# A decoder layer on one core: the null key and value subtracted in the fold, scores in two banks, gate in the banks of the transposes

## The reference

```
x = x + q * scan(sigmoid(a), kv)             # [q, kv, a] = norm(layernorm(x)) @ w_qkva
x = x + layernorm(attention(layernorm(x), context)) * ln_scale + ln_bias
x = x + bitlinear(silu(bitlinear(xn, w_gate)) * bitlinear(xn, w_up), w_down)   # xn = layernorm(x)
```

```
k = concat(null_k, k); v = concat(null_v, v)       # 65 rows
attn = softmax(q k^T / 8);  out = concat_heads(attn v) @ Wout
```

## Time and profile before

| what | value |
|---|---|
| three runs | 515.12, 511.77, 512.62 us; median 512.62 |
| span of the profiled execution | 510.8 us (the profile gives no other time of it) |
| PE busy | 476.4 us, 93% |
| DVE busy | 416.6 us, 82% |
| ACT busy | 334.4 us, 65% |
| POOL busy | 314.1 us, 61% |
| chain that ended last | PE 74%, DVE 11%, POOL 4%, DMA 3%, issue 3% |

### The profile page before, as it was taken

The page is one execution under the profiler, slowest core; times in us unless marked ns, Lnnn a source line. Parts: engine busy times, 40 slices in busy tenths (PEclk is TensorE's granted clock), DMA queues, the critical chain, the costliest instruction groups (busy, mean ns, idle before and its releaser), DMA issues.

```text
span 510.8 us, 8856 instructions
## 1 busy us (share of the span) xinstructions
PE 476.4 (93%) x2934; PEld 390.5 (76%) x2962; DVE 416.6 (82%) x933; ACT 334.4 (65%) x461; POOL 314.1 (61%) x486
## 2 busy tenths in 40 slices
PE   1999999999997998999999999999999999999774
PEld 0778888877676887888888888888888888887432
DVE  4789898968437558799999899898998998997786
ACT  3556652245333334788888888888897888787562
POOL 2234546510003457788787887887878778788861
PEclk9999999999999999999999999999999999999979
DMA  8996000320000000011122211313132212221234
GB/s 256 324 360 255 3 0 1 72 52 2 0 1 1 1 1 7 6 27 42 36 52 45 50 39 38 58 42 49 36 50 46 53 37 52 44 52 37 63 85 117
DMA packets 67116, 31.80 MB, mean 62 GB/s; under 512 B 49664, under 2 KB 65280, under 8 KB 67072
## 3 DMA queue, kind: packets, MB, share of 16 engines
q1 hardware_dynamic: 67072, 31.24, 24.5%
HBM read 15.24 MB, written 4.19 MB: 38 GB/s over the span
## 4 chain that ended last, share of the span: by engine, by line
PE 74%; DVE 11%; POOL 4%; DMA 3%; issue 3%; SPq 2%; ACT 2%; DVEq 0%; POOLq 0%; ACTq 0%
PE psum L1270 33%; PE psum L1534 10%; PE psum L1539 9%; PE psum L1286 9%; DMA xs<-in_x_dram 3%; PE psum L1510 2%; PE psum L1518 2%; SPq L397 2%; PE psum L1412 2%; PE psum L1391 1%; PE psum L1305 1%; DVE den L1080 1%; PE psum L1374 1%; DVE region_d L1071 1%; DVE mx L1068 1%
## 5 line engine op out<-in xcount | busy, mean ns | idle before, releaser
L554 POOL TENSOR_TENSOR region_d<-region_d,rden 128x1024 f32<-128x1024 f32 x32 | 60.9, 1903 | 74.9 <-DVE rden L1085 74.9
L1270 PE MATMUL psum<-Mhi,xT2hi 128*128 128x260 f32 x256 | 75.9, 297 | 0.2
L1270 PE MATMUL psum<-Mlo,xT2hi 128*128 128x260 f32 x256 | 72.9, 285 | 0.0
L1270 PE MATMUL psum<-Mhi,xT2lo 128*128 128x260 f32 x256 | 72.9, 285 | 0.0
L1534 PE MATMUL psum<-VW,region_d 128*128 128x256 f32 x256 | 61.2, 382 | 3.2 <-DVE pTn L1174 3.2
L1539 PE MATMUL psum<-VW,region_d 128*128 128x256 f32 x256 | 60.5, 379 | 0.0
L1534 PEld LDWEIGHTS psum<-VW,region_d 128*128 128x128 f32 x256 | 48.3, 191 | 13.1 <-DVE pTn L1174 4.5
L1068 DVE TENSOR_REDUCE mx<-psum 128x8 f32<-128x520 f32 x64 | 44.5, 696 | 13.0 <-PE psum L1270 11.4
L1539 PEld LDWEIGHTS psum<-VW,region_d 128*128 128x128 f32 x256 | 48.6, 190 | 6.6
L1093 DVE SCALAR_TENSOR_TENSOR region_c<-psum,zw,region_c 128x1024 f32<-128x1024 f32 x32 | 41.0, 1283 | 12.5 <-ACT region_c L768 10.9
L1270 PEld LDWEIGHTS psum<-Mhi,xT2hi 128*128 128x128 f32 x256 | 48.7, 190 | 1.3 <-issue 0.9
(11 more groups left out here) (151 smaller groups left out, 1217.5 us busy)
## 6 DMA issues: line engine op xcount, KB each, us to landing
out_dram<-xs SPq DMA_DIRECT2D x32, 128.0 KB, 1.9
xs<-in_x_dram SPq DMA_DIRECT2D x1, 2560.0 KB, 13.4
VW<-in_L_xattn_Wkv_dram SPq DMA_DIRECT2D x1, 2048.0 KB, 12.2
region_b<-in_L_xattn_Wkv_dram SPq DMA_DIRECT2D x1, 2048.0 KB, 18.4
xs<-in_x_dram SPq DMA_DIRECT2D x3, 512.0 KB, 7.4
region_w<-in_L_ffn_w_gate_dram SPq DMA_DIRECT2D x2, 512.0 KB, 10.3
region_w<-in_L_ffn_w_up_dram SPq DMA_DIRECT2D x2, 512.0 KB, 7.7
region_w<-in_L_ffn_w_down_dram SPq DMA_DIRECT2D x8, 128.0 KB, 5.1
```

What stands on the lines that cost most here:

```text
L554: pool.tensor_tensor(p2[:, v, 0:H * MK].rearrange("p (h j) -> p h j", j=MK), e[:, :, 0:MK], rden[:, v, :].unsqueeze(2).broadcast_to([P, H, ...
L1270: mm = pe.matmul(dst, lhsT, rhs, start=i == 0, stop=i == len(terms) - 1)
```

## The change: what it does

With the null key subtracted from every key, the null score is 0, and softmax is the same: all scores of a row shift by one number. With the null value subtracted from every value, the output lacks a constant row, the null value times Wout, since the probabilities sum to 1. So ACT's copy in `put_kvT` becomes one with a bias, minus the null key or value of each row:

```diff
-                act.activation(kvT[:, i % 4, :], bank(i % 2, BM), ACT.Copy).then_inc(kvT_ready, 1)
+                null = 0 if i < HC else 1
+                act.activation(kvT[:, i % 4, :], bank(i % 2, BM), ACT.Identity, bias=nulls_neg[:, null:null + 1]) \
+                    .then_inc(kvT_ready, 1)
```

The 65th columns go: scores have 64 columns a head, 8 heads fill a bank, and a tile's scores are 12 matmuls of 128x512 into banks 0 and 1. Softmax shifts by max(maximum, 0) in one instruction that gives shift minus score, ACT's exponential has scale -1, and a small DVE instruction writes the null column of both halves:

```diff
             def softmax_half(n, hh, u):
 
-                scores = banks(2 * hh, 2)[:, :, 0:HB * J].rearrange("p b (h j) -> p b h j", j=J)
+                scores = bank(hh).rearrange("p (h j) -> p h j", j=MK)
+                e = e2[:, u, hh * HB * J:(hh + 1) * HB * J].rearrange("p (h j) -> p h j", j=J)
                 dve.wait_ge(sim_psum, 2 * n + hh + 1)
                 if hh == 0:
-                    if positive(2 * n - 2):
-                        dve.wait_ge(p_ready, 2 * n - 2)
-                dve.tensor_reduce(mx[:, hh, :].rearrange("p (b h) -> p b h", h=HB), scores, AX.X, ALU.max) \
-                    .then_inc(max_done, 1)
+                    if positive(n):
+                        dve.wait_ge(shift_done, n)
...
-                dve.tensor_tensor(
-                    e2[:, u, hh * 2 * HB * J:(hh + 1) * 2 * HB * J].rearrange("p (b h j) -> p b h j", b=2, j=J),
-                    scores,
-                    mx[:, hh, :].rearrange("p (b h) -> p b h", h=HB).unsqueeze(3).broadcast_to([P, 2, HB, J]),
-                    ALU.subtract).then_inc(sim_sub, 1)
+                if hh == 1:
+                    null = e2[:, u, :].rearrange("p (r h j) -> p r h j", r=2, j=J)[:, :, :, MK]
+                    dve.tensor_scalar(null, mx[:, :, :], 0.0, None, ALU.max).then_inc(shift_done, 1)
+                dve.scalar_tensor_tensor(out=e[:, :, 0:MK], in0=mx[:, hh, :].unsqueeze(2).broadcast_to([P, HB, MK]),
+                                         scalar=0.0, in1=scores, op0=ALU.max, op1=ALU.subtract).then_inc(sim_sub, 1)
```

The constant row is added on TensorE by a product of ones with `vnull` (hi part in one row, rest in another), now the first of the products in bank 7; the null transpose, its copies and the last product go:

```diff
@@ -1517,27 +1498,27 @@
                         at = (HC // 2 + i) * P
                         mm = pe.transpose(psum[:, 5, i * P:(i + 1) * P], p2[:, u, at:at + P], ident[:, :])
                     mm.then_inc(pT1_psum, 1)
-                    if positive(n):
-                        pe.wait_ge(y2_ready, n)
-                    if n == 0:
-                        pe.wait_ge(vwn_ready, 1)
-                    pe.transpose(psum[0:NP, 7, D:D + P], p2[:, u, H * MK:], ident[:, :]).then_inc(pTn_psum, 1)
                 if filling(n):
                     scores_half(n + 2, 1, (u4 + 2) % 4, half(n + 2 - u), batch(n + 2))
                 if exists(n + 2, T) and exists(n - 5, T):
                     gate_up(n, v)
                 if exists(n, T):
 
-                    pe.wait_ge(pTn_ready, n + 1)
+                    if positive(n):
+                        pe.wait_ge(y2_ready, n)
+                    if n == 0:
+                        pe.wait_ge(vnull_ready, 1)
+                    pe.matmul(bank(7, D), ones_r[:, :], vnull[:, :], start=True, stop=False)
                     pe.wait_ge(pT0_ready, n + 1)
                     for pair in range(HC // 2):
...
 
                     pe.wait_ge(pT1_ready, n + 1)
                     for pair in range(HC // 2, HC):
-                        pe.matmul(bank(7, D), pT[:, pair, :], VW[:, batch(n), pair, :], start=False, stop=False)
-                    pe.matmul(bank(7, D), pTn[:, :], VWnull[:, :], start=False, stop=True).then_inc(out_psum, 1)
+                        mm = pe.matmul(bank(7, D), pT[:, pair, :], VW[:, batch(n), pair, :], start=False,
+                                       stop=pair == HC - 1)
+                    mm.then_inc(out_psum, 1)
```

`vnull` is made by one matmul from the sum of Wout over the pairs of heads, which POOL forms:

```diff
             groups(stage1)
+            pool.wait_ge(nvsel_zero, 1)
+            for row in (0, DH // 2):
+                pool.tensor_copy(nvsel[:, row:row + 1], nulls[:, 1:2]).then_inc(nv_set, 1)
+            pool.wait_ge(wout_loaded, 16)
             pool.wait_ge(q_psum, NG)
-            pool.memset(nvsel, 0.0).then_inc(nvsel_zero, 1)
+            pool.tensor_tensor(wsum, wout[:, 0, :], wout[:, 1, :], ALU.add).then_inc(wout_summed, 1)
+            for pair in range(2, HC):
+                pool.wait_ge(wout_summed, pair - 1)
+                pool.tensor_tensor(wsum, wsum, wout[:, pair, :], ALU.add).then_inc(wout_summed, 1)
...
-            def null_values(first, end):
-
-                pe.wait_ge(nv_set, 2 * HC)
-                for pair in range(first, end):
-                    mm = pe.matmul(psum[0:NP, 7, 0:D], nvsel[:, pair * NP:(pair + 1) * NP], wout[:, pair, :],
-                                   start=pair == 0, stop=pair == HC - 1)
-                return mm
+            def null_values():
+
+                pe.wait_ge(nv_set, 2)
+                pe.wait_ge(wout_summed, HC - 1)
+                pe.matmul(psum[0:NR, 7, 0:D], nvsel[:, :], wsum, start=True, stop=True).then_inc(vnull_psum, 1)
```

`null_key` and the 16 copies of `null_values` go from DVE's part of the fold (removed functions, L995 to L1018), and with them the waits on them. Scores keep banks 0 and 1, up has banks 2 and 3, gate takes banks 4 and 5 behind the copies of T0 and T1 in the tiles up to n = 29, and stands behind up:

```diff
@@ -1444,22 +1416,14 @@
             def scores_half(n, hh, u4, q, b):
 
                 pe.wait_ge(xT2_lo_ready, q + 1)
-                if n == 0 and hh == 1:
-                    pe.wait_ge(vw_first, HC)
-                    pe.wait_ge(vw_second, HC)
                 if positive(2 * n - 1 + hh):
                     pe.wait_ge(sim_sub, 2 * n - 1 + hh)
-                if positive(n - 7):
-                    pe.wait_ge((silu_ready, h_ready)[hh], n - 7)
-                for g in (2 * hh, 2 * hh + 1):
-                    mm = group(bank(g, HB * J),
-                               [(xT[:, (u4 // 2) % 2, k, (u4 % 2) * P:(u4 % 2 + 1) * P],
-                                 m[:, k, b, g * HB * J:(g + 1) * HB * J])
-                                for k in range(KD) for xT, m in ((xT2hi, Mhi), (xT2hi, Mlo), (xT2lo, Mhi))])
-                mm.then_inc(sim_psum, 1)
+                group(bank(hh), [(xT[:, (u4 // 2) % 2, k, (u4 % 2) * P:(u4 % 2 + 1) * P],
+                                  m[:, k, b, hh * HB * MK:(hh + 1) * HB * MK])
+                                 for k in range(KD) for xT, m in ((xT2hi, Mhi), (xT2hi, Mlo), (xT2lo, Mhi))]) \
+                    .then_inc(sim_psum, 1)
 
...
+                if positive(n - 4):
+                    pe.wait_ge(silu_ready, min(n - 4, T - 7))
...
             def gate_up(n, slot, down_between=None):
 
                 pe.wait_ge(nT_ready[slot], 16 * ((n - 5) // 2 + 1))
-                pe.wait_ge(sim_sub, upto(2 * n + 5, 2 * T))
+                def up():
+
+                    if positive(n - 5):
+                        pe.wait_ge(h_ready, n - 5)
+                    for j in range(2):
+                        mm = group(bank(2 + j), [(nT3[:, slot, k, :], wuT[:, k, j * 512:(j + 1) * 512]) for k in range(KD)])
+                    mm.then_inc(up_psum, 1)
+
+                if n < T - 2:
+                    up()
+                else:
+                    pe.wait_ge(sim_sub, 2 * T)
                 if positive(n - 5):
                     pe.wait_ge(silu_ready, n - 5)
                 for j in range(2):
-                    mm = group(bank(j), [(nT3[:, slot, k, :], wgT[:, k, j * 512:(j + 1) * 512]) for k in range(KD)])
+                    if n < T - 2:
+                        pe.wait_ge((pT0_ready, pT1_ready)[j], n + 1)
+                    mm = group(bank(gate_bank(n) + j),
+                               [(nT3[:, slot, k, :], wgT[:, k, j * 512:(j + 1) * 512]) for k in range(KD)])
                 mm.then_inc(gate_psum, 1)
-                mm.then_inc(up_psum, 1)
+                if n >= T - 2:
+                    up()
...
                 if exists(n, T):
 
-                    pe.wait_ge(p_ready, 2 * n + 2)
+                    if n == 0:
+                        pe.wait_ge(vw_first, HC)
+                        pe.wait_ge(vw_second, HC)
+                    pe.wait_ge(p_ready, n + 1)
                     if positive(n):
                         pe.wait_ge(pT0_ready, n)
+                    if positive(n - 5):
+                        pe.wait_ge(silu_ready, min(n - 5, T - 7))
```

More of the change, by code:

```diff
@@ L1485, in gate_up @@
                     down(down_between, T)
-                pe.wait_ge(sim_sub, upto(2 * n + 6, 2 * T))
-                if positive(n - 5):
-                    pe.wait_ge(h_ready, n - 5)
-                for j in range(2):
-                    mm = group(bank(2 + j), [(nT3[:, slot, k, :], wuT[:, k, j * 512:(j + 1) * 512]) for k in range(KD)])
-                mm.then_inc(up_psum, 1)
+                if n >= T - 2:
+                    up()
             def stages2_3(n, u4):
```

186 lines of the change are left out of this document (77 added, 109 removed).

## The result

The changed kernel takes 498.62 us in the median of four runs (497.85 to 499.26) against 513.48 for the kernel before on the same occasion (511.77 to 515.12): 0.9701 of it, 95% interval 0.967 to 0.9731. The forecast was 497.5. The profiled execution after spans 496.7 us where the one before spans 510.8.

What follows compares the result with a forecast made beforehand. PE was taken as the bound, with DVE 6% behind. The terms 6.75 + 4.4 + 2.6 + 0.9 + 0.5 = 15.15 us off the 510.8 us span give 495.65, plus 1.8 for the median: 497.5 us, range 492 to 504.5.

Steps and rivals of the forecast that it cites:

- Steady tiles: Tiles n = 5 to 29, bound by PE: 0.27 us less a tile, 6.75 us in all (5.5 to 8.7).
- Merging: Scores on PE: twelve matmuls of 512 columns in place of 24 of 260 gain 0.16 us a tile (0.13 to 0.26).
- gate would cost no wait: Gate's second half, in its new place, follows ACT's copy of T1 with a slack of at least 0.24 us.
- the slower rival: DVE's fused difference takes two passes, 1.40 us in place of 0.70, and DVE becomes the bound: 521.0 us, chance 0.05.
- n = 1 to 4: Early tiles, where out mostly waits for DVE's null correction: -4.4 us (-2 to -5) once it goes.
- the null write: DVE's new write of the null column, 128x16, priced by a small product: +0.20 us a tile (0 to 0.28).
- n = 0: First tile: the second score half moves into PE's wait for the constant row: -2.6 us (-1.5 to -3.5).
- the half clock: PE's 1.2 GHz level in the first tile: lasting through out, it would cost up to 1.7 us more.
- The 0.36 us: In the first tile, out might start 0.36 us earlier, since POOL's small product no longer stands before DVE's release.
- Fold: Stretch before the first tile: less waiting for DVE's difference, -1.0, and -0.1 more, -0.9 us with the biases (0 to -1.3).
- the new wait of 1.6 us: On PE ahead of the last fold_values, a wait for ACT's copies replaces the eight null products, some 1.6 us.
- Tail: Tiles 30 and 31 give 2 x 0.27 us: -0.5 us (0 to -1.5).

Runs made afterwards that it cites:

- null_by_reduce: The changed kernel with the null write on DVE as a tensor_reduce in place of the tensor_scalar: 495.48 us, 0.9635 of the kernel before.
- after_again: The changed kernel unaltered, timed and traced again on another occasion: 499.06 us, 0.9698 of the kernel before.

## Why the prediction was right, and where its sizes were off

**Steady tiles.** The bound was read rightly: PE's own work, shown by a transposition that costs three quarters of its length and a DVE instruction of 0.69 us that costs nothing in the period. The term was 0.27 a tile and came as 0.293. Merging was sized well by the two pitches (0.16 against 0.14), though a matmul fewer saved 8.7 ns where the prediction read 12 to 14. From T1 to out a tile takes the same as before, 2.28 against 2.27, since the ones stand where the null transposition stood; what is gone is the null product behind out. From out's second half to the next scores an odd tile takes 2.52 in place of 2.65 and an even one 3.06 in place of 3.29; why the even ones, with `pair_T` there, gain 0.1 more stays open. That gate would cost no wait was right: in the tile that starts at 287.19 ACT's copy of T1 ends at 291.77 and gate's second half begins at 292.22, 0.45 later, where 0.24 at least was forecast, and the other order shows what the place is worth: 0.56 us of wait ahead of up, none behind it. The difference as a scalar_tensor_tensor cost 0.02 us less than the plain one, not 0.05 more; the slower rival is refuted.

**Head.** n = 1 to 4: -4.46 against -4.4, of which 2.94 were the correction; the rest is not divided by a run. That it came so close is in part luck: the null write held this stretch up by 0.83 us, and without it, in null_by_reduce, the gain is 5.3, beyond the term's range of 2 to 5. n = 0: -2.91 against -2.6; the half clock did not return, which the forecast left open. The 0.36 us that the constant row might come earlier did not show, since the null write took them: as a reduce it lets the row come 13.37 us after tile 0's first scores, in place of 13.70.

**Fold.** -0.92 against -0.9, with the new wait of 1.6 us for ACT where it was put.

**The term that was mis-sized is the null write**, "+0.20 (0 to 0.28)". It took 0.50 in the mean and up to 1.72, because I priced it by the nearest small product, of one column, which took 0.21 beside POOL in the kernel before and never stood beside POOL's long product. It cost 1.2 us in the head. The Trainium skill has the rule that I didn't look up: "SBUF — State Buffer", section "Who interferes with whom", says that a tensor_scalar in a two-port mode and a GpSimd instruction lock each other out of a shared pair of ports for a whole instruction, and that on trn2 a tensor_reduce never does. The runs agree: 1.50 beside POOL's product, with an end 0.04 us behind POOL's, and 0.188 in every tile as a reduce.

**Tail.** -0.5 was forecast for tiles 30, 31 and the rest; about -0.2 is left when the last steady tile's 0.29 is taken off the table's -0.45. One pair of traces can't settle this term: in after_again, the same kernel, the stretch is 1.6 us longer, with a granted clock of 0.66 in its last 10 us, where the first trace has 1.00 there and 0.83 in the 10 us before.

**Sum.** Of the 1.1 us between 497.5 and 498.62, 0.86 lie in the kernel before, whose median was 512.62 in the three runs that the forecast started from and 513.48 in the four of the comparison. The gain is 14.86 us where the terms gave 15.15. In the two traces the terms' stretches gained 15.77; the start and the last store, +1.7 together, took it back to 14.1. So in these traces the closeness of the sum is in part luck: what the start and the last store lost stands against terms that gained more than forecast.

## What to carry to other kernels

On the engine that bounds a stretch, price every instruction by the distance of two starts, and count instructions as well as columns: here one fewer of a pair saved 8.7 ns. A small instruction on an engine that isn't the bound can still hold a stretch up when it stands in order between two others, as the 0.28 us correction did for 2.94 us in four tiles; look for it in the part of the program where the pipeline fills. Before adding a small DVE instruction, see what POOL runs at that moment, and choose a form that doesn't have to wait for it.
